# An attention and mixture-of-experts block: causal masks move from TensorE's matmuls to a fused add-and-minimum on DVE

## The reference

```python
sim = jnp.einsum('bhid,bhjd->bhij', q, k)                 # q is scaled by 64 ** -0.5
mask_value = -jnp.finfo(sim.dtype).max
causal_mask = jnp.triu(jnp.ones((n, n), dtype=bool), k=1)
sim = jnp.where(causal_mask, mask_value, sim)
attn = jax.nn.softmax(sim.astype(jnp.float32), axis=-1)
...
adj = jnp.clip(attn.reshape(b * HEADS, n, n) + jnp.eye(n), 0.0, 1.0)
deg = jnp.sum(adj, axis=-1, keepdims=True)
```

## Time and profile before

| | |
|---|---|
| median of 3 runs | 1265.96 us (1265.9 to 1266.74) |
| the profiled execution | 1259.73 us, span 1258.0 |
| PE busy | 1165.9 us, 93% |
| ACT busy | 879.4 us, 70% |
| DVE busy | 845.2 us, 67% |
| POOL busy | 499.8 us, 40% |
| granted clock of PE | 0.99 of full speed |

### The profile page before, as it was taken

The page is one execution under the profiler, slowest core; times in us unless marked ns, Lnnn a source line. Parts: engine busy times, 40 slices in busy tenths (PEclk is TensorE's granted clock), DMA queues, the critical chain, the costliest instruction groups (busy, mean ns, idle before and its releaser), DMA issues.

```text
span 1258.0 us, 27195 instructions
## 1 busy us (share of the span) xinstructions
PE 1165.9 (93%) x7808; PEld 877.3 (70%) x7808; DVE 845.2 (67%) x3507; ACT 879.4 (70%) x2671; POOL 499.8 (40%) x641
## 2 busy tenths in 40 slices
PE   5999999999999999999999999999999997898994
PEld 4676767667676767676767676767676764888993
DVE  5647585858676776767676767675757688566556
ACT  5768686868686868686777777777768683655662
POOL 5405152524343343435242525252525160354444
PEclk9999999999999999999999999999999999999997
DMA  7940000000000000000000000000000003122227
GB/s 216 406 164 1 1 6 4 4 4 2 6 0 8 0 8 0 8 0 8 0 8 0 8 0 8 0 8 0 8 0 8 0 9 87 35 61 58 65 63 212
DMA packets 37246, 46.84 MB, mean 37 GB/s; under 512 B 6010, under 2 KB 28540, under 8 KB 37201
## 3 DMA queue, kind: packets, MB, share of 16 engines
q1 hardware_dynamic: 32880, 37.81, 9.5%
q0 software_dynamic: 4320, 8.47, 2.0%
HBM read 18.14 MB, written 28.58 MB: 37 GB/s over the span
## 4 chain that ended last, share of the span: by engine, by line
PE 55%; DVE 22%; issue 7%; POOL 7%; ACT 6%; DMA 1%; DVEq 0%; ACTq 0%; SPq 0%; POOLq 0%
PE bank L595 48%; DVE eb L1251 4%; DVE nmax L1238 3%; DVE ea L1248 3%; POOL slots L502 2%; POOL eb L488 2%; ACT gt L980 2%; ACT eb L1019 2%; PE bank L896 2%; DVE aT L1267 2%; POOL ea L486 2%; PE bank L678 1%; PE bank L702 1%; DVE dT L1261 1%; PE bank L681 1%
## 5 line engine op out<-in xcount | busy, mean ns | idle before, releaser
L486 POOL TENSOR_TENSOR ea<-ea,wgt 128x256 f32<-128x256 f32 x128 | 85.9, 671 | 437.6 <-DVE wgt L1256 437.3
L1238 DVE TENSOR_REDUCE nmax<-bank 128x2 f32<-128x256 f32 (+1 forms) x256 | 140.0, 552 | 92.9 <-PE bank L595 92.7
L595 PE MATMUL bank<-kT,qT 128*128 128x256 f32 (+1 forms) x512 | 200.6, 487 | 0.0
L595 PEld LDWEIGHTS bank<-gt,vnat 128*64 128x64 f32 x1024 | 62.1, 136 | 105.8 <-issue 47.8
L1035 ACT ACTIVATE f1T<-z,gb 128x256 f32<-128x256 f32 x128 | 65.0, 508 | 100.8 <-DVE z L1307 98.9
L488 POOL TENSOR_TENSOR eb<-eb,wgt 128x512 f32<-128x512 f32 x128 | 132.9, 1038 | 0.0
L1019 ACT ACTIVATE eb<-bank,nmax 128x256 f32<-128x256 f32 x256 | 119.1, 471 | 16.2 <-DVE nmax L1238 7.1
L1019 ACT ACTIVATE ea<-bank,nmax 128x128 f32<-128x128 f32 x256 | 91.8, 363 | 53.4 <-DVE nmax L1238 52.5
L980 ACT ACTIVATE gt<-bank 128x512 f32<-128x512 f32 (+1 forms) x256 | 112.8, 501 | 23.1 <-PE bank L681 22.6
L595 PE MATMUL bank<-gt,vnat 128*64 128x256 f32 (+1 forms) x1024 | 111.5, 339 | 17.4 <-ACT gt L980 17.4
L1251 DVE SCALAR_TENSOR_TENSOR eb<-idw,ssum,eb 128x256 f32<-128x256 f32 x256 | 113.5, 481 | 0.0
(11 more groups left out here) (233 smaller groups left out, 3199.8 us busy)
## 6 DMA issues: line engine op xcount, KB each, us to landing
slots<-zero SPq DMA_DIRECT2D x33, 520.0 KB, 15.1
zin<-slots SPq DMA_DIRECT2D x71, 65.0 KB, 1.8
got<-pairs SPq DMA_DIRECT2D x8, 512.0 KB, 7.5
raw_gu<-in_guT SPq DMA_DIRECT2D x8, 352.0 KB, 3.0
out<-x_all SPq DMA_DIRECT2D x8, 256.0 KB, 2.7
pairs<-zout,zin POOLq DMA_INDIRECT x71
dn<-in_downT SPq DMA_DIRECT2D x2, 512.0 KB, 16.0
slots<-z,row_now POOLq DMA_INDIRECT x64
```

Of the source, the lines that this page charges most:

```text
L486: nc.gpsimd.tensor_tensor(ea[:, s], ea[:, s], wgt[:, s, 0:2].unsqueeze(2).to_broadcast([P, 2, P]), ALU.mult)
L595: return nc_mm(o, st, mo, start=first, stop=last, **more)
L1238: V.tensor_reduce(nmax[:, n % 3, 2 * t:2 * t + 2], bank[1 + t][:, 0:2 * width].rearrange("p (a j) -> p a j", a=2), X, ALU.max, negate=True ...
```

## The change

The mask matmuls go from PE, and with them the bf16 identity, the bf16 mask and their casts on DVE. Keys are copied with the scale negated, so that the banks hold negated scores. `hide` is a 128 x 256 tile: zeros left, +3e38 above the diagonal right. `maxima` becomes, for each tile and head, one fused instruction (`tensor_tensor_reduce`): it adds `hide` to the bank, writes the sum to `ea` or `eb`, and keeps the row minimum, that is the negated row maximum, which a second instruction writes to `nmax`. The exponentials read `ea` and `eb` in place of the bank, with scale -1, and write in place. In front of each pair of fused instructions stands a semaphore increment on DVE (`k_turn`), which carries the wait for PE. PE's waits for the exponentials are as before.

```diff
-MASKED = -3.0e38
+MASKED = 3.0e38
...
-        maskf = at("maskf", [P, P])
+        spare = at("spare", [P, P])
...
-        ident_bf = at("ident_bf", [P, P], bf16)
-        mask = at("mask", [P, 2, P], bf16)
+        hide = at("hide", [P, 2 * P])
...
-            sp.wait_ge(k_casts, 2)
+            sp.wait_ge(k_casts, 1)
...
-            nc.gpsimd.memset(maskf[:, :], 0.0)
+            nc.gpsimd.memset(hide[:, :], 0.0)
...
-            nc.gpsimd.affine_select(out=maskf[:, :], in_=maskf[:, :], compare_op=ALU.is_ge, fill=MASKED,
+            nc.gpsimd.affine_select(out=hide[:, P:], in_=hide[:, P:], compare_op=ALU.is_ge, fill=MASKED,
...
                 q, k = qT[:, n % 2], kT[:, n % 2]
-                product(bank[1][:, 0:2 * P], ident_bf[:, :], mask[:, :, :], True, False)
-                product(bank[1][:, 0:2 * P], q[:, xt(0)], k[:, :, xt(0)], False, True).then_inc(s_s.sem, 1)
+                product(bank[1][:, 0:2 * P], q[:, xt(0)], k[:, :, xt(0)], True, True).then_inc(s_s.sem, 1)
                 if n >= 1:
                     a_exp.wait(pe, b, 2 * n)
-                sb1 = bank[2][:, :].rearrange("p (h j) -> p h j", h=2)
-                product(sb1[:, :, xt(1)], ident_bf[:, :], mask[:, :, :], True, False, skip_group_check=True)
-                product(bank[2][:, :], q[:, xt(1)], k[:, :, :], False, True,
-                        skip_group_check=True).then_inc(s_s.sem, 1)
+                product(bank[2][:, :], q[:, xt(1)], k[:, :, :], True, True).then_inc(s_s.sem, 1)
...
-            pe.wait_ge(k_casts, 1)
...
-                    done = copy(kT[rows, n % 2, a, :], bank[0][rows, TOKENS:], scale=SCALE)
+                    done = copy(kT[rows, n % 2, a, :], bank[0][rows, TOKENS:], scale=-SCALE)
...
-                    done = nc.scalar.activation(e[:, s, a, :], bank[1 + t][:, a * width:(a + 1) * width], ACT.Exp,
+                    done = nc.scalar.activation(e[:, s, a, :], e[:, s, a, :], ACT.Exp, scale=-1.0,
                                                 bias=nmax[:, s, i:i + 1], accum_out=ssum[:, s, i:i + 1])
...
             def maxima(b, n, t):
                 s_s.wait(dve, b, 2 * n + 1 + t)
+                V.sem_inc(k_turn, 1)
                 width = (t + 1) * P
-                V.tensor_reduce(nmax[:, n % 3, 2 * t:2 * t + 2],
-                                bank[1 + t][:, 0:2 * width].rearrange("p (a j) -> p a j", a=2), X, ALU.max,
-                                negate=True).then_inc(d_max.sem, 1)
+                for a in range(2):
+                    i = 2 * t + a
+                    done = V.tensor_tensor_reduce((eb if t else ea)[:, n % 3, a, :],
+                                                  bank[1 + t][:, a * width:(a + 1) * width], hide[:, (1 - t) * P:],
+                                                  1.0, MASKED, ALU.add, ALU.min, nmax[:, n % 3, i:i + 1])
+                done.then_inc(d_max.sem, 1)
...
-            mask_casts()
+            dve.wait_ge(k_ident, 1)
```

More of the change, by code:

```diff
@@ L291, in build_program @@
         s_down, d_zout = Signal(sem("s_down"), 1), Signal(sem("d_zout"), 1)
-        k_gu, w_out = sem("k_gu"), sem("w_out")
+        k_gu, w_out, k_turn = sem("k_gu"), sem("w_out"), sem("k_turn")
         def xt(t):
@@ L555, in _ @@
             pool.wait_ge(k_vlow, 2)
-            pool.wait_ge(k_casts, 2)
+            pool.wait_ge(k_casts, 1)
             pool.wait_ge(k_fold, 3)
@@ L1014, in exps @@
                 d_max.wait(act, b, 2 * n + 1 + t)
-                s, width = n % 3, (t + 1) * P
+                s = n % 3
                 e = eb if t else ea
@@ L1157, in low_weights @@
                                 ALU.subtract).then_inc(k_low, 1)
-            def mask_casts():
-                dve.wait_ge(k_ident, 1)
-                V.tensor_copy(ident_bf[:, :], ident[:, :])
-                for a in range(2):
-                    done = V.tensor_copy(mask[:, a, :], maskf[:, :])
-                done.then_inc(k_casts, 1)
             def before_cast():
```

## The result

The kernel with the change takes **1344.88 us** (median of 4 runs, 1340.14 to 1345.18), the kernel before 1266.35 in the same session: a ratio of 1.0609, 95% interval [1.0584, 1.0634]. It is slower by 78 us. The forecast was 1301, with a range from 1274 to 1344; the median lies 0.9 us above that range.

A forecast was written before the change was run, and what follows sets the result against it. A closed DVE-ACT-DVE loop, about tied with PE's circuit, was taken to bound phase 1 (4.38 us a step). Batch terms 28.6, 5.2 and 1.5 gave +35 us: 1295 from the profiled 1259.7, 1301 as median; range 1274 to 1344.

The forecast's parts named there:

- rival 1: PE bounds phase 1 after all, so two mask matmuls fewer per pair give 29 us: 1237 us; chance 8%.
- the loop's term: Phase 1 steps bounded by the DVE-ACT loop: fused maxima and SBUF-reading exponentials lengthen each from 4.38 to 4.89 us, +0.51.
- Step 3: Fourth pair-of-heads step of a phase 1 batch, filled by DVE's own routing work: forecast +0.41 us.
- Step 5: Sixth pair-of-heads step of a phase 1 batch, filled by DVE's own routing work: forecast +0.41 us.
- Step 1: Second step of a phase 1 batch, maxima right behind adjacency: forecast +0.54 us in all, exponentials included.
- step 0: First step of a phase 1 batch: all four exponentials lie on the path behind ACT's table load, +0.14 us.
- Step 2: Third step of a phase 1 batch: DVE's waits for PE vanish, so the accumulated shift falls back to about +0.04 us.
- my lower bound: Fused instructions in the maxima as cheap as a reduction of their length, exponentials at nothing: +8 us, 1274 us.
- Rival 4: The fused instruction in the maxima is cheap, at the lower end of the range: 1274 us, still slower; chance 8%.
- the tail: End of a batch's phase 1: last adjacency 2.4 us late, 0.16 us slack, so 2.2 us pass on into phase 2.
- rival 2: In the maxima, fused instructions do not overlap with their neighbours: the upper bound, 1344 us; chance 15%.
- Rival 3: PE pauses 0.5 us more per step, so the clock falls; phase 2 at 0.83 adds 70 us, about 1370; chance 4%.

The follow-up runs named there:

- e6: The kernel before plus only the semaphore increment k_turn in front of each maxima, DVE's loop head at slot 0: 1269.33 us, ratio 1.0024.
- e1: The changed kernel with only DVE's loop head moved to slot 0 of its 256-instruction block: 1281.33 us, ratio 1.0134 to the kernel before.
- e3: The kernel before, without the change, its DVE loop head moved to slot 239 of a block: 1322.85 us, ratio 1.0461.
- e14: The changed kernel with loop head at slot 0 and dT and aT of pair n-3 moved behind the second maxima of pair n: 1304.62 us, ratio 1.0322.

## Why the prediction was wrong

**The direction and the loop were right.** DVE, ACT, DVE bounds the steps without routing, and each comparison of the prediction between what hides and what shows held: PE's two matmuls are worth 4 us and not 29 (rival 1), and only in step 2; the early bank is worth nothing; `k_turn` is hidden in the loop steps.

**The size of the loop's term was too large.** This is the smaller of the two failures, and it points the other way. The nearest row for the fused instruction was L1248 and L1251 with 0.25, 0.27 and 0.41 from start to start; it took 0.21 and 0.33, which is the lower part of my bounds. Forecast for a loop step +0.51, measured +0.24 to 0.25: first maxima +0.09 for +0.19, second +0.08 for +0.25, exponentials +0.07 for +0.07. Over a batch 0.8 for 2.2. Step 3, forecast +0.41, got nothing: its maxima are some 0.17 longer, and behind them a TENSOR_SCALAR of the routing, 0.56 long in the kernel before, is 0.37 long, for a reason that no run shows. Step 5 got 0.18 for 0.41. Step 1 got 0.39 (4.24 for 3.85) where its own share of the forecast was 0.40 (0.54 less the 0.14 of step 0), and that is luck: the fused pairs cost it 0.17 for 0.33, and `k_turn`, costed at nothing, makes its first maxima 0.16 later (1.80 behind the reciprocal for 1.64), since in this step no instruction covers it (in e6, with `k_turn` alone, the step is 0.12 longer). Step 2 gave back 0.59 (4.43 for 5.02), a little more than forecast. The kernel without the stall, 1281 (e1), lies between my forecast and my lower bound. Rival 4, the cheap instruction, given 8%, had come nearest to the truth of the instruction.

**What failed is the passage from batch to batch.** The sum lets "2.2 us pass into the tail, and from there into phase 2" and has no term for DVE's jump back to the head of its loop: it was put at nothing without a reason, under the statement that "nothing else on DVE moved". The runs showed 5.1 us a pass there, 61 us in all. I costed instructions by their time on the engine and never as places in its code. The fused pairs with their accumulator reads, and `k_turn`, make DVE's body longer by 64 instructions (306 for 242) and shift its head by 125; where it now lies, DVE stands still for 4.6 us a pass (54.8 in 12) and PE's clock falls (26 us more of PE busy time than in e1, 1182.5 for 1156.3). The two overlap in part, since together they make 61 us between the profiled spans of e1 and of the kernel (1276.9 and 1338.1), 5.1 for each of 12 passes. The diff shows instructions, not their place; but the program could have been counted. By the block rule a body of 276 fits if it begins at place 236 of a block or before, and one of 340 only up to place 172, so both its length and its head mattered. The Trainium skill's rule on taken branches (the page named above) was the rule against this change that I should have weighed; the same section says that the fetch of straight code is mostly hidden. On this the trace agrees: DVE's straight code ahead of the loop, up to 130 us, has no wait called issue.

**The median landed at the edge of the range for another reason than that edge stood for.** 1344 was the price of fused instructions without overlap (rival 2); they overlap. Rival 3 had the right sign: PE pauses and the clock falls. But the pause is not 0.5 us a step, it is 4.6 us a batch, and the granted clock is 0.80 and 0.86 in two windows, not in all of phase 2. The sign that the prediction had named for rival 3, a clock below 1.00 in the batches, came true, and with q14 it was the trace's plainest sign that something else had happened. That forecast and time differ by only 44 us is luck too: a loop term some 20 us too large stands against a missing one of 61.

## What to carry to other kernels

Count the instructions of a loop's body per engine, the accumulator reads too, before one instruction becomes several, and the instructions ahead of it, which set where its head lies. Where head and end of the body no longer lie in two blocks of 256, the back edge cost some 5 us here, and a fixed place of the head or a hint on the back edge gave it back. A wait "<- issue" at the first instruction of a loop, as often as the loop goes back, with more packets on the queue that carries instructions, is how it looks. And idle time of an engine in a closed loop is not free to be filled: dT and aT put into 1.16 us of it cost 23 us. The trace shows PE waiting for aT and dT stretched beside POOL; which of the two costs more no run tells.

## What the hardware showed that I had not expected

- The stall is nearly the same in both kernels: 2.6 us a pass at L1307 of the kernel before (31.7 in 12, e3), 2.7 at L1298 after, and where the loop first stood a second one of 1.9 (22.7 in 12) a few instructions on. That second gap is gone at slot 200, and no run explains it. Nor is it explained why a head at slot 150 or 200 has a gap of 2.6 to 2.8 us at the entry into the loop, once, and one at slot 0 or 239 has not.
- A TENSOR_TENSOR whose operands all lie in SBUF, dT, is stretched beside POOL's work. dT by its durations, minimum, median, maximum, in e1 and then in e14:

```profile
L1252 DVE TENSOR_TENSOR dT<-gvT,vT x128: 393/395/427, 32.3 to 1052.4; 128x256 f32<-128x256 f32 x128
```

```profile
L1252 DVE TENSOR_TENSOR dT<-gvT,vT x128: 393/432/1203, 34.6 to 1076.5; 128x256 f32<-128x256 f32 x128
```

  aT, with one operand in a bank, stays at 424 to 426 in e14, and so does the fused instruction at 527.51 in the rows of e14, under the same multiplication of POOL. The Trainium skill (GPSIMD Engine Reference, Specifications) says that POOL's way to SBUF is shared with DVE for instructions with two SBUF inputs; the trace agrees, with up to 0.8 us on one instruction.
- The fused add and minimum with its accumulator read costs its engine 0.21 us for 128 and 0.33 for 256 elements, less than the SCALAR_TENSOR_TENSOR of the same size (0.25 and 0.41), though it reads a bank.
